# Layer normalisation applied on ScalarE instead of VectorE, and the rounding constant of the second quantisation added on GpSimd, in a two-layer transformer kernel on one core

## The reference

```
x = x + _L0_attn_ref(_layernorm(x, axis=-1), ...)   # 16 heads of 8, gated relative bias
x = x + _L0_ffn_ref(_layernorm(x, axis=-1), ...)    # 16 experts, 4 of them per token, and a shared one
x = x + _L1_attn_ref(_layernorm(x, axis=-1), ...)   # 8 heads of 64
x = x + _L1_ffn_ref(_layernorm(x, axis=-1), ...)    # FP4 linears
```

```
scale = max(|block|) / 6;  q = nearest of {0, .5, 1, 1.5, 2, 3, 4, 6} to |block / scale|, times sign, times scale
gate, y = fp4_linear(x, w_gate), fp4_linear(x, w_up);  h = silu(gate) * y;  return fp4_linear(h, w_down)
```

## Time and profile before

| | us |
|---|---|
| median of 3 runs (2319.95 to 2324.96) | 2321.24 |
| profiled execution, its own time | 2319.1 |
| its span | 2317.3 |
| TensorE busy | 2037.8 (88%) |
| VectorE busy | 1625.4 (70%) |
| ScalarE busy | 1308.5 (56%) |
| GpSimd busy | 1000.9 (43%) |

### The profile page before, as it was taken

The page is one execution under the profiler, slowest core; times in us unless marked ns, Lnnn a source line. Parts: engine busy times, 40 slices in busy tenths (PEclk is TensorE's granted clock), DMA queues, the critical chain, the costliest instruction groups (busy, mean ns, idle before and its releaser), DMA issues. The chain is left out here.

```text
span 2317.3 us, 56731 instructions
## 1 busy us (share of the span) xinstructions
PE 2037.8 (88%) x18115; PEld 1061.5 (46%) x18115; DVE 1625.4 (70%) x3414; ACT 1308.5 (56%) x2072; POOL 1000.9 (43%) x867
## 2 busy tenths in 40 slices
PE   5569999999999999983999759999999999998566
PEld 3434444444444444453555323444444444443345
DVE  4778888888888888866544676666666666664696
ACT  2236666666666666642222346777778787877121
POOL 1133222322322332421000226787878787877454
PEclk9779999999999999976999988999999999999787
DMA  5522212221222221100000271111111111100000
GB/s 134 149 62 56 53 48 53 54 50 50 55 52 48 54 54 49 37 11 1 1 0 0 92 232 36 42 31 38 34 34 37 31 38 31 41 14 1 1 14 23
DMA packets 126924, 106.60 MB, mean 46 GB/s; under 512 B 39636, under 2 KB 102724, under 8 KB 126860
## 3 DMA queue, kind: packets, MB, share of 16 engines
q1 hardware_dynamic: 124640, 103.37, 16.8%
q10 hardware_dynamic: 2220, 2.45, 0.4%
HBM read 75.81 MB, written 29.53 MB: 45 GB/s over the span
## 5 line engine op out<-in xcount | busy, mean ns | idle before, releaser
L1049 DVE TENSOR_REDUCE b_mx<-psum 128x1 f32<-128x512 f32 x1024 | 663.9, 686 | 143.3 <-PE psum L868 81.0
L1033 ACT ACTIVATE b_prob<-psum 128x1024 f32<-128x1024 f32 x512 | 523.9, 1023 | 317.9 <-PE psum L900 317.8
L1736 POOL TENSOR_TENSOR f_plo<-f_prob,f_phi 128x512 f16<-128x512 f32 x512 | 586.5, 1156 | 164.4 <-ACT f_phi L1861 140.1
L1879 DVE TENSOR_REDUCE f_mx<-psum 128x1 f32<-128x512 f32 x512 | 328.7, 683 | 169.1 <-PE psum L1756 168.1
L1860 ACT ACTIVATE f_prob<-psum 128x512 f32<-128x512 f32 x512 | 307.3, 600 | 150.8 <-PE psum L1767 149.7
L948 PE MATMUL psum<-b_prob,b_v 128*32 128x256 f32 x4096 | 327.4, 391 | 1.6 <-ACT b_prob L1033 0.5
L1861 ACT ACTIVATE f_phi<-psum 128x512 f16<-128x512 f32 x512 | 306.0, 598 | 0.0
L804 POOL COPY b_v<-v 128x64 f32 x64 | 15.1, 236 | 596.1 <-PE psum L948 595.7
L900 PE MATMUL psum<-b_diag,b_toep 128*128 128x79 f16 (+1 forms) x4224 | 266.6, 208 | 0.0
L807 POOL TENSOR_TENSOR b_diag<-flip,grev 128x1024 f16<-128x1024 f16 x128 | 239.6, 1892 | 0.0
L900 PEld LDWEIGHTS psum<-b_diag,b_toep 128*128 128x128 f16 x4224 | 235.2, 99 | 9.0 <-issue 2.6
(11 more groups left out here) (301 smaller groups left out, 3432.4 us busy)
## 6 DMA issues: line engine op xcount, KB each, us to landing
d_qk<-e_qk SPq DMA_DIRECT2D x64, 256.0 KB, 2.6
b_toep<-d_line SPq DMA_DIRECT2D x128, 64.0 KB
f_qa<-d_qk SPq DMA_DIRECT2D x64, 128.0 KB, 2.9
f_ka<-d_qk SPq DMA_DIRECT2D x64, 128.0 KB, 2.9
b_q<-d_q SPq DMA_DIRECT2D x128, 54.0 KB
d_k<-a_qk SPq DMA_DIRECT2D x48, 128.0 KB, 2.3
b_toep<-d_line SPq DMA_DIRECT2D x128, 32.0 KB
b_q<-b_m SPq DMA_DIRECT2D x256, 1.0 KB
```

The costliest lines, as they stand in the source:

```text
L1033: nc.scalar.activation(prob[:, t % 4, :].rearrange("p (a n) -> p a n", a=2), ps[:, EXP + 2 * (t % 2):EXP + 2 * (t % 2) + 2, :], ACT.Exp).t ...
L1049: nc.vector.tensor_reduce(mx[:, b, t, half:half + 1], ps[:, bank, :], AX.X, ALU.max).then_inc(s.max_read, 1)
L1736: nc.gpsimd.tensor_tensor(plo[:, t % 4, at], prob[:, t % 4, at], phi[:, t % 4, at], ALU.subtract).then_inc(s.plo_ready, 1)
L1879: nc.vector.tensor_reduce(mx[:, b, t, half:half + 1], ps[:, MAX + half, :], AX.X, ALU.max).then_inc(s.max_read, 1)
```

## The change

VectorE no longer applies the normalisation. GpSimd computes beside rstd also shift = -mean * rstd, with two more instructions on 128x4, and ScalarE computes xn = rstd * x + shift with four Identity activations per chunk, whose scale and bias are columns in on-chip memory. `normalise` moves from VectorE's list into ScalarE's: in project0 to the start of each step, in project1 and quant_ffn to the front of the list, in output0 behind move_aT. In quant_ffn the add of the second quantisation moves from VectorE (`quant_h`) to GpSimd (`finish_h`).

```
 def norm_rstd(nc, g, ln, pool, n, u, s):
+    pool.wait_ge(s.xn_ready, done(n - 2))
     nc.gpsimd.tensor_tensor(ln.rstd[:, u, :], ln.mv[:, u, :, 1], g.lnc[:, 0, :], ALU.add).then_inc(s.eps_added, 1)
+    nc.gpsimd.tensor_tensor(ln.shift[:, u, :], ln.mv[:, u, :, 0], g.lnc[:, 2, :], ALU.mult)
...
     nc.gpsimd.tensor_tensor(ln.rstd[:, u, :], ln.rstd[:, u, :], g.lnc[:, 1, :], ALU.pow).then_inc(s.eps_added, 1)
+    pool.wait_ge(s.eps_added, done(2 * n + 1))
+    nc.gpsimd.tensor_tensor(ln.shift[:, u, :], ln.shift[:, u, :], ln.rstd[:, u, :], ALU.mult).then_inc(s.rstd_ready, 1)
 
-def norm_apply(nc, ln, x, n, u, xn_ready):
+def norm_apply(nc, ln, x, n, u, act, rstd_ready, xn_ready):
+    act.wait_ge(rstd_ready, done(n))
     for k in range(CT):
-        last = nc.vector.tensor_scalar(ln.xn[:, u, k, :], x[...], ln.mv[:, u, k, 0:1], ln.rstd[:, u, k:k + 1], ALU.subtract, ALU.mult)
+        last = nc.scalar.activation(ln.xn[:, u, k, :], x[...], ACT.Identity, bias=ln.shift[:, u, k:k + 1], scale=ln.rstd[:, u, k:k + 1])
...
# project0, ScalarE
                 def step(n, u, last):
+                    if not last:
+                        apply(n + 1, 1 - u)
                     act.wait_ge(s.gates_psum, done(n))
...
# output0, ScalarE
-                pipeline(act, [(4, move_xT), (1, move_aT), (5, score)])
+                pipeline(act, [(4, move_xT), (1, move_aT), (3, normalise), (5, score)])
# project1, ScalarE
-                pipeline(act, [(2, lambda n, u: high(n, u, FIRST)), (1, move_xT), (2, lambda n, u: high(n, u, REST))])
+                pipeline(act, [(1, normalise), (2, lambda n, u: high(n, u, FIRST)), (1, move_xT), (2, lambda n, u: high(n, u, REST))])
# quant_ffn
-                pipeline(act, [(2, gates), (4, move_hT), (1, move_xT)])
+                pipeline(act, [(1, normalise), (2, gates), (4, move_hT), (1, move_xT)])
...
                 def finish_h(n, u):
...
-                    quantise_end(nc.gpsimd, hq[...], CT * FI // QB, th[u], chain(pool, s.hq_rounded, END_LINKS * n)).then_inc(s.hq_ready, 1)
+                    link = chain(pool, s.hq_rounded, (1 + END_LINKS) * n)
+                    link(quantise_add(nc.gpsimd, CT * FI // QB, th[u]))
+                    quantise_end(nc.gpsimd, hq[...], CT * FI // QB, th[u], link).then_inc(s.hq_ready, 1)
...
                 def quant_h(n, u):
-                    link(quantise_start(nc.vector, hid[...], CT * FI // QB, th[u], link))
-                    quantise_add(nc.vector, CT * FI // QB, th[u]).then_inc(s.hq_begun, 1)
+                    quantise_start(nc.vector, hid[...], CT * FI // QB, th[u], chain(dve, hchain, START_LINKS * n)).then_inc(s.hq_begun, 1)
```

More of the change, by code:

```diff
@@ L336, in norm_scratch, with norm_stats @@
     ln.gap = sb("gap", [P, 1])
+    ln.shift = sb("shift", [P, 2, CT])
     ln.xn = sb("xn", [P, 2, CT, E])
     return ln
-def norm_stats(nc, ln, x, n, u, link, var_ready):
+def norm_stats(nc, ln, x, n, u, link, dve, rstd_ready, var_ready):
     for k in reversed(range(CT)):
@@ L346, in norm_stats @@
     link(last)
+    dve.wait_ge(rstd_ready, done(n - 2))
     nc.vector.memset(ln.gap[:, :], 0.0)
@@ L350, in norm_stats, with norm_rstd @@
     last.then_inc(var_ready, 1)
[L353 to L358, removed]
-def norm_apply(nc, ln, x, n, u, xn_ready):
+def norm_rstd(nc, g, ln, pool, n, u, s):
+    pool.wait_ge(s.var_ready, done(n))
+    pool.wait_ge(s.xn_ready, done(n - 2))
+    nc.gpsimd.tensor_tensor(ln.rstd[:, u, :], ln.mv[:, u, :, 1], g.lnc[:, 0, :], ALU.add).then_inc(s.eps_added, 1)
+    nc.gpsimd.tensor_tensor(ln.shift[:, u, :], ln.mv[:, u, :, 0], g.lnc[:, 2, :], ALU.mult)
+    pool.wait_ge(s.eps_added, done(2 * n))
+    nc.gpsimd.tensor_tensor(ln.rstd[:, u, :], ln.rstd[:, u, :], g.lnc[:, 1, :], ALU.pow).then_inc(s.eps_added, 1)
+    pool.wait_ge(s.eps_added, done(2 * n + 1))
+    nc.gpsimd.tensor_tensor(ln.shift[:, u, :], ln.shift[:, u, :], ln.rstd[:, u, :], ALU.mult).then_inc(s.rstd_ready, 1)
+def norm_apply(nc, ln, x, n, u, act, rstd_ready, xn_ready):
+    act.wait_ge(rstd_ready, done(n))
     for k in range(CT):
-        last = nc.vector.tensor_scalar(ln.xn[:, u, k, :], x[:, bass.ds(n * CT + k, 1), :].rearrange("p a e -> p (a e)"),
-                                       ln.mv[:, u, k, 0:1], ln.rstd[:, u, k:k + 1], ALU.subtract, ALU.mult)
+        last = nc.scalar.activation(ln.xn[:, u, k, :], x[:, bass.ds(n * CT + k, 1), :].rearrange("p a e -> p (a e)"), ACT.Identity,
+                                    bias=ln.shift[:, u, k:k + 1], scale=ln.rstd[:, u, k:k + 1])
     last.then_inc(xn_ready, 1)
@@ L481, in move_xT, with apply @@
                     nc.scalar.copy(xT[:, u, :], ps[:, TX + u, :]).then_inc(s.xT_ready, 1)
+                def apply(n, u):
+                    act.wait_ge(s.x_turned, done(n - 2))
+                    norm_apply(nc, ln, g.x, n, u, act, s.rstd_ready, s.xn_ready)
+                act.wait_ge(g.x_loaded, 16)
+                apply(0, 0)
                 move_xT(0, 0)
                 def step(n, u, last):
+                    if not last:
+                        apply(n + 1, 1 - u)
                     act.wait_ge(s.gates_psum, done(n))
@@ L2052, in move_hT, with normalise @@
                         nc.scalar.copy(hqT[0:y_ - x, u, c, :], ps[0:y_ - x, TH + (F3 * u + c) % 2, :]).then_inc(s.hT_ready, 1)
-                pipeline(act, [(2, gates), (4, move_hT), (1, move_xT)])
+                def normalise(n, u):
+                    act.wait_ge(s.xq_begun, done(n - 2))
+                    norm_apply(nc, ln, g.x, n, u, act, s.rstd_ready, s.xn_ready)
+                pipeline(act, [(1, normalise), (2, gates), (4, move_hT), (1, move_xT)])
             @block.tensor
@@ L2150, in persistent @@
     g.bvo = sb("bvo", [P, 2, E])
-    g.lnc = sb("lnc", [P, 2, CT])
+    g.lnc = sb("lnc", [P, 3, CT])
     g.v = sb("v", [P, NT, E])
```

71 lines of the change are left out of this document (30 added, 41 removed).

## The result

The changed kernel took 2362.61 us (median of 4, 2355.96 to 2371.7), the kernel before, run beside it, 2323.1 (2319.95 to 2326.06): a ratio of 1.0173, 95% interval 1.0135 to 1.021. Slower was forecast, but 2328 and at most 2337. The profiled execution took 2362.56 us (span 2360.8) against 2319.1 (span 2317.3).

A forecast was written before the change was run, and what follows sets the result against it. The prediction took VectorE, blocked by GpSimd's long instructions, to bound quant_ffn, and SyncE's store queue project0. Terms 1.4 + 0.7 + 0.6 + 4.1 = +6.8 on 2319.1 gave 2325.9, with the median's 2.1 forecast as 2328; range 2315 to 2337.

The forecast's parts named there:

- The chance of "slower": Whole kernel: 0.53 that it measures slower, against 0.29 for the same and 0.18 for faster.
- project0, +1.4: project0: first store 1.4 us late through later rstd, Identities and table loads, the rest hidden behind SyncE's queue; bounds +0.8, +3.
- rival 2: VectorE bounds project0 and project1 after all: -7 and -3 us there, total 2316; chance 0.07.
- Four Identities, 1.5 us: ScalarE's four normalising activations per chunk, not in the trace, taken as 1.5 us from between 1.05 and 2.8.
- rival 3: Handovers cost more in quant_ffn, period 19.8 us, 2334, chance 0.15; or project0's table load costs twice, +2.8, 2331, chance 0.05.
- output0, +0.7: output0: ScalarE's applications fit into waits for TensorE's transposes, only the last step is later: +0.7 us, bounds 0 and +2.
- project1, +0.6: project1: first store some 1.4 us later, six turns win 0.7: +0.6 us, bounds -2 and +2.5.
- the -0.7: project1: six turns of 4.12 us become 4.0 at best, since the Identities fit ScalarE's 1.63 us of idle time.
- Theory A, moved tiles: attend0 and attend1: moved tiles or the added work itself lengthened them; with moved tiles 875 and 768 us, span about 2351.
- quant_ffn, +4.1: quant_ffn: fill -1.3, five periods together +0.8, end +4.6 us; bounds 0 and +9.
- Rival 1: quant_ffn: VectorE passes beside GpSimd's adds, GpSimd's own work bounds; five periods 3.6 us shorter, total 2309; chance 0.12.
- theory R: TensorE's attend0 loop: whether the ninth code fetch starts ahead of the jump back decides on refetching, 7.5 us a turn.

The follow-up runs named there:

- experiment 3: Kernel before with 101 unused semaphore increments ahead of ScalarE's attend1 loop: 2338.52 us (1.0047); changed kernel with 155 there: 2337.03 us (1.0048).
- experiment 5: Kernel before with only ScalarE's normalisations in quant_ffn, add left on VectorE: 2311.66 us (0.9957); second kernel, plus 96 and 160 TensorE increments: 2348.41 us (1.0107).
- experiment 1: Kernel before with the change in quant_ffn alone, tiles as in the changed kernel: 2330.66 us (1.0031).
- experiment 2: Kernel before with only the add of quant_ffn's second quantisation moved from VectorE to GpSimd: 2332.51 us (1.0066).
- experiment 4: Kernel before with TensorE increments, 96 ahead of attend0 and 160 ahead of attend1: 2357.1 us (1.0147); 256 ahead of attend0 only: 2360.08 us (1.0154).
- experiment 6: Changed kernel rerun: 2357.29 us; with e_qk copies before project1's normalisation: 2367.76; kernel before with quant_ffn normalisations and 48 TensorE increments in attend0: 2417.55.
- experiment 7: 96 TensorE increments in attend0: kernel before 2323.72 us; changed kernel, plus 155 on ScalarE in attend1, 2337.74; kernel before with quant_ffn normalisations 2314.08.

## Why the prediction was wrong, and where it was right

Of 43.5 us of span, 15.3 are ScalarE's attend1 loop on a bad place, 16.3 TensorE's attend0 loop (two renewed fetches, whose number differs from execution to execution), 9.5 the change's own in four stages, and 2.1 the start of project0, whose first statistics come between 34.4 and 38.7 us from one profile to the next whatever the kernel.

**The step that failed** is the one that wasn't there. The sum had terms for the four stages that the diff touches and none for the two attention stages, as if code that doesn't change takes a time that doesn't change; they brought 16.3 and 15.3 us. It left out that instructions added to ScalarE's list move every later loop of ScalarE, which is shown to be worth the 15.3 (experiment 3, both ways). Of the 16.3 the runs show what they are, renewed fetches of TensorE's loop, and not that the change brought them. The chance of "slower" came true mostly for another reason than mine, so its coming true is in good part luck. (Its sum, 0.46 x 0.7 + 0.2, is 0.52, not 0.53.) The order of ScalarE's instructions would have told that the loop moves, but no row of the kernel before told what that costs: it had no fetch inside attend1. Its second fetches in attend0 could have been seen in the spread of more executions, which three didn't show.

**project0, +1.4**: +1.4 (14.9 against 13.5), step by step as told: the copy at 44.69, two table loads of 1.28 around 1.65 us of Identities, and the store. The ten other profiles with the old project0 have 13.5 to 13.9, so +0.9 to +1.4. The last store is late by 0.9 to 1.6, so the queue was the bound; rival 2 falls.

**Four Identities, 1.5 us**: 1.65, 0.48 us for one alone.

```profile
41.83 1.65 ACT L372 ACTIVATE a_xn<-x,a_shift,a_rstd 128x128 f32<-128x128 f32 x4 [8.51 <-POOL a_shift L365]
...
45.29 1.28 ACT L372 ACT_TABLE_LOAD   x1
46.59 1.65 ACT L372 ACTIVATE a_xn<-x,a_shift,a_rstd 128x128 f32 x4
```

1.6 is what the Trainium skill's formula gave (ScalarE: Activation LUTs, What ACT_TABLE_LOAD costs), and by that the trace agrees with the page. The load is followed by an activation 0.02 us after its end: no drain, so the second half of rival 3 falls. Its first half falls too: the period in quant_ffn is 18.47, not 19.8.

**output0, +0.7**: +2.0 to +2.3 in the two pairs of the table, just beyond its bound of 2, and more than that at a like clock. With the old output0 the stage takes 46.5 to 46.6 us where the clock granted in it is 0.61 (five profiles), 43.8 to 44.3 at 0.69 to 0.70 (four) and 43.4 at 0.78 (two); with the new one 48.4 to 48.8 at 0.64 and 47.2 at 0.68: some 3 us more. Part of it is GpSimd's, which the forecast did not count: its copy of the attention result (c_at), for which TensorE's transposes wait, stands behind the longer rstd and shift and starts 1.1 us later in the first step (7.3 us after the stage's first product with wT, before 6.2). The rest wasn't taken apart.

**project1, +0.6**: +3.1 to +3.9, beyond its bound of 2.5. The late first store, +1.4, came as told. The sign of the steady turns was wrong: 8.9 us each in place of 8.6. The half with the Identities still takes 4.1 us where I had 4.0, and the half with the statistics 4.7 to 4.9 where I had 4.4. I let the Identities fill 1.63 us in which ScalarE waits for the ring; they fill it wholly (1.65 us), and VectorE then waits for the copy behind them. ScalarE in the changed kernel, then VectorE:

```profile
1367.45 0.56 ACT L1566 CAST e_qk<-psum 128x512 f16<-128x512 f32 x1
```

```profile
1363.92 2.60 DVE L1614 TENSOR_TENSOR e_qk<-psum,e_qk 128x512 f16<-128x512 f32 x4
1368.05 2.92 DVE L1614 TENSOR_TENSOR e_qk<-psum,e_qk 128x512 f16<-128x512 f32 x4 [1.53 <-ACT e_qk L1566]
```

The first row is ScalarE's copy, made right behind its Identities; VectorE waits 1.53 us for it, where it did its own applications before. So the -0.7 didn't come. But the turn is as long without the Identities and without GpSimd's longer chain, so it doesn't need them: in the five profiles with ScalarE's normalisations in quant_ffn alone, where project1's code is the old one, the same four turns take 35.2 to 35.3 us, in four with the whole change 35.3 to 35.5, and in the six with neither these normalisations nor their tiles 34.5. The rows under experiment 5 show such a turn. What is common to the longer ones is the larger lnc, the shift tiles and one memset on VectorE; which of them it is, and how, is open. Theory A, moved tiles, fell for attend1 in experiment 1 and is open here.

**quant_ffn, +4.1**: +2.7 (+3.5 with good places). The fill won 1.55 us (forecast 1.3), the last two periods cost 1.6 each (forecast 1.5), the end 2.0 (1.6). The five periods ahead of them gave 0.9 back where I had +0.8: 18.47 in place of 18.8. The first quantisation ended 10.75 us into the period, as told (10.7); behind it hh's L615 was held up by 0.5 us (0.89 in place of 0.41), where I had 0.9. A profile of another kernel with the old quant_ffn has 180.5 us (experiment 3) where four have 177.7 to 178.1, so single profiles of this stage can differ by as much as the term. The exclusion between the two engines is shown by experiments 2 and 5: the addition alone +12.5, the normalisations alone -8.9, their sum +3.6. Rival 1, the weaker exclusion, falls.

**Open:** why TensorE's loop at its unshifted place is fetched anew in 0 to 2 turns of a profile. The eighth fetch came 56.7 us after the first product with V in the profile of before and 57.4 us in the changed one, where a ninth stood at the jump back, at 65.7; that the two race is a reading of these rows. The time of the eighth doesn't tell the cases apart: 57.0 without a renewed fetch (the first kernel of experiment 5), 56.6 and 56.8 with one (experiments 3 and 2). And at 96 theory R's outcome came without its reason: there the ninth fetch came at 62.3, some 3 us ahead of the jump back, and nothing was fetched anew. Each renewed turn brought nine packets or so (18 more for two, 126 or 127 for 14). Experiments 4, 6 and 7 show that the place decides (48 always, 96 never, 0 and 256 sometimes), not what happens at it. The Trainium skill (Runtime: NRT & Kernel Launch, Instruction fetch mechanics) says that code comes in blocks of 256 instructions, the next one while the present one runs, and that a taken branch to a block that isn't held waits for a DMA. The return of the behaviour at 256, and ScalarE's at 615 and 871, agree with 256. No run here shows how many blocks are held.

## What to carry to other kernels

An instruction added anywhere ahead of a hot loop, on the same engine, may cost more in that loop than where it stands: compare the stages that a change doesn't touch, and the packets of the instruction queues, before pricing the ones that it does. A loop on a bad place shows as idle time that ends on "issue", once per turn; semaphore increments in idle time, behind the ones others wait for, move it, and their number must be tried (48 made it far worse, 96 mended it).

Before a stage's slowdown is put down to the work moved into it, look at that stage in a kernel that has the change's tiles and not its work: project1's turn was as long there.

Between VectorE and GpSimd, move work away from VectorE that would lie beside GpSimd's long instructions, and don't give GpSimd another long one: here the first won 8.9 us and the second lost 12.5, and together they looked like a change that does little.

## What the runs showed of the hardware

- A loop whose code is fetched anew costs 7.6 us a turn on TensorE (5.1 of them standstill; 48 increments) and 1.9 to 2.6 on ScalarE (11.1 to 15.3 over the 6 jumps back that its 7 turns have); the fetches themselves are 16 KB and 8 KB packets, 0.1% of the DMA engines' time (0.5% where every turn fetched), so no share of busy time shows them.
- The same code can be fetched once or several times from one execution to the next: on one chip 25 us of spread in 21 of 23 executions of the kernel before, 5 after 96 instructions were put ahead of one loop.
- A semaphore increment on TensorE takes 0.155 us (96 of them start from 114.4 to 129.1 us).
- The same output0 took 46.5 us at a granted clock of 0.61, 43.8 at 0.70 and 43.4 at 0.78.
- A VectorE instruction of 0.18 us took 2.62 beside GpSimd's 3.16 us ones, and GpSimd's own kept their length.
